# One copy of each pixel instead of two: VectorE takes the odd columns of every patch, and the edge columns move into the rows of the other offsets

## The reference, cut to what matters

```
xs = jnp.concatenate([x] + [_shift(x, s) for s in shifts], axis=1)     # five copies, 15 channels
t = xs ... reshape(B, h * w, PATCH * PATCH * C5)
tn = (t - mu) * jax.lax.rsqrt(var + EPS) * ln_gamma + ln_beta
h = jnp.einsum('bnp,pd->bnd', tn, W) + b
h = jnp.concatenate([h, text], axis=1)                                 # 228 tokens
h = h + attention(layernorm(h)); h = h + ffn(layernorm(h))
```

## Time and profile before

| | |
|---|---|
| median of 3 runs | 1894.72 us (1888.71 to 1895.52) |
| the profiled execution | 1889.4 us, span 1887.7 us |
| mean granted TensorE clock | 0.88 |
| PE busy | 1579.8 us (84%) |
| PEld busy | 1297.6 us (69%) |
| DVE busy | 1364.8 us (72%) |
| ACT busy | 1283.7 us (68%) |
| POOL busy | 1089.7 us (58%) |
| patch matmuls that read `pix` (L1092) | 2048 instructions, 408.4 us |
| DMA | 132.96 MB, of which 118.32 MB read from HBM |

### The profile page before, as it was taken

How to read it: one execution, slowest core, us unless ns; L and a number is a source line. 1 busy time by engine, 2 the same in 40 slices (tenths; PEclk the granted TensorE clock), 3 DMA queues, 4 the chain that set the end, 5 groups by cost and what they waited for, 6 DMA issues and landing times.

```text
span 1887.7 us, 50796 instructions
## 1 busy us (share of the span) xinstructions
PE 1579.8 (84%) x16574; PEld 1297.6 (69%) x16574; DVE 1364.8 (72%) x3151; ACT 1283.7 (68%) x1958; POOL 1089.7 (58%) x1503
## 2 busy tenths in 40 slices
PE   0539999999999999999999999999466666666666
PEld 0427788888888888888888888887345555555555
DVE  3636676767767676767676767676389999999996
ACT  1226666766767676767676666665288888888887
POOL 5035555555555555555555555554177777777775
PEclk9869999999999999999999999999666666666665
DMA  8674666665657565756565666660000000000000
GB/s 102 141 127 59 95 87 96 86 99 83 103 79 104 83 99 83 99 88 94 89 94 91 91 93 88 94 87 25 17 16 21 21 21 22 22 22 22 22 22 26
DMA packets 159967, 132.96 MB, mean 70 GB/s; under 512 B 32558, under 2 KB 151040, under 8 KB 159808
## 3 DMA queue, kind: packets, MB, share of 16 engines
q1 hardware_dynamic: 159168, 131.00, 44.4%
q0 software_dynamic: 768, 1.57, 0.5%
HBM read 118.32 MB, written 11.91 MB: 69 GB/s over the span
## 4 chain that ended last, share of the span: by engine, by line
PE 66%; DVE 15%; issue 7%; SPq 3%; ACT 3%; DMA 3%; POOL 1%; DVEq 1%; ACTq 0%; POOLq 0%
PE ps L1092 20%; PE ps L1176 8%; PE ps L1259 7%; PE ps L1250 7%; PE ps L1206 4%; DVE ff_st L860 4%; PE ps L1238 3%; PE ps L1232 3%; PE ps L1211 3%; PE ps L1336 2%; PE ps L1355 2%; DVE xpix L841 2%; PE ps L1167 2%; DVE xpix L853 1%; PE ps L1157 1%
## 5 line engine op out<-in xcount | busy, mean ns | idle before, releaser
L1092 PE MATMUL ps<-w_eff,pix 118*112 118x193 f32 (+1 forms) x2048 | 408.4, 337 | 25.0 <-ACT pix L909 24.3
L927 ACT ACTIVATE probs<-ps,isw 116x688 f32<-116x688 f32 x384 | 299.2, 831 | 171.6 <-PE ps L1238 171.6
L527 POOL TENSOR_TENSOR xpix<-probs,g_b 112x192 f32<-112x192 f32 (+1 forms) x512 | 296.5, 609 | 109.1 <-ACT probs L1044 99.7
L741 DVE TENSOR_REDUCE nmax<-ps 116x12 bf16<-116x1344 f32 (+2 forms) x192 | 299.6, 1560 | 80.2 <-PE ps L1211 77.7
L452 POOL TENSOR_TENSOR xsq<-xsq 118x784 f32<-118x784 f32 (+2 forms) x192 | 221.8, 1155 | 218.5 <-ACT xsq L920 208.4
L1092 PEld LDWEIGHTS ps<-w_eff,pix 118*112 118x112 f32 (+1 forms) x2048 | 309.8, 167 | 52.4 <-issue 18.9
L472 POOL TENSOR_SCALAR_AFFINE_SELECT probs<-probs 116x464 f32<-116x464 f32 x384 | 268.2, 717 | 46.5 <-ACT probs L927 31.0
L909 ACT ACTIVATE pix<-xpix 118x896 f32<-118x896 f32 (+1 forms) x128 | 198.4, 1552 | 104.9 <-DMA xpix<-in_x 56.0
L457 POOL TENSOR_TENSOR front_st<-front_st,expo 128x2 f32<-128x2 f32 x64 | 45.0, 703 | 235.2 <-DVE front_st L693 221.2
L1336 PE MATMUL ps<-w1t,xpix 96*112 96x384 f16 (+1 forms) x512 | 160.7, 488 | 14.6 <-ACT xpix L1035 13.3
L685 DVE TENSOR_SCALAR front_st<-ps 112x1 f32<-112x1 f32 (+1 forms) x128 | 18.3, 151 | 213.8 <-PE ps L1157 202.4
(11 more groups left out here) (161 smaller groups left out, 3363.3 us busy)
## 6 DMA issues: line engine op xcount, KB each, us to landing
xpix<-in_x SPq DMA_DIRECT2D x192, 196.0 KB
xpix<-in_x SPq DMA_DIRECT2D x192, 195.1 KB
rden<-den_rows SPq DMA_DIRECT2D x256, 85.5 KB, 2.1
out<-xpix SPq DMA_DIRECT2D x64, 87.0 KB
out<-xpix SPq DMA_DIRECT2D x64, 84.0 KB
xpix<-in_x SPq DMA_DIRECT2D x128, 34.1 KB
xpix<-in_x SPq DMA_DIRECT2D x128, 34.0 KB
den<-o_sb SPq DMA_DIRECT2D x256, 2.7 KB
```

What stands on the lines that cost most here:

```text
L527: last = nc.gpsimd.tensor_tensor(v2[0:P, b, tile, cols], gel[0:P, b, tile, cols], g2_b[0:P, cols], ALU.mult)
L741: V.tensor_reduce(dst, src, AX_X, ALU.max, negate=True).then_inc(s_mx, 1)
L927: A(probs[0:TB, g, 2 * e:2 * e + 2, :], ps[0:TB, 4 + 2 * e:6 + 2 * e, 0:SK], ACT.Exp, scale=isw[0:TB, 7:8]).then_inc(s_p, 1)
L1092: last = MM(ps_tok[tile][0:P, :], src, w_eff[0:HI, o, :], start=(o == 0), stop=(o == OFFS - 1))
```

## The change

- **Loads.** Each pixel is loaded once: `load_pixels` issues five DMAs instead of ten. Both images' pixels share one tensor `xpix`, the even image in partitions 0 to 53 and the odd one in 64 to 117 (`UP` = 64).
- **Regrouping.** `pix` is two buffers in turn. ACT copies the even columns to rows 0 to 53 (`regroup_even`, the same two shapes of 8 x 112 and 8 x 84 elements in each partition), and DVE the odd columns to rows 64 to 117 (new `regroup_odd`, one copy of 8 x 196 = 1568 elements in each partition, behind maxima round 2). Both are for image n+4 in step n; ACT's copy of tile 1 moves from the start of the next step to behind copy_maxima.
- **Edges.** The 2 x 48 edge pixels of a patch no longer have an offset of their own. POOL gathers them in one copy (`sides`, 48 partitions x 2 x 182), now at the end of its step for image n+4, and two SP DMAs (`place_sides`) put them into six further rows of each half of `pix` (`EDGE` = 6, 6 rows x 8 offsets = 48). A matmul has 124 rows, and an image has 8 offsets x 2 tiles, 32 instructions; P4 goes from 14 to 13 (of 16). ACT has one square less (L917), POOL one add less (`ADDS` = 3).
- **Broadcast.** The inverse denominators go to 17 rows of each head's 32 instead of 32; `rden` is filled with ones once.
- **Start-up.** The scratch of the setup moves out of `xpix`, so image 1 is loaded right behind image 0; DVE's setup gets the odd copy of image 0 (behind the patch weights, before READY1) and, behind the text rows, that of image 1. The edge weights are moved by two DMAs.

```diff
-OFFS = PATCH // 2 + 1
-LO, HI = CH * (PATCH + 2), 64 + CH * (PATCH + 2)
+OFFS = PATCH // 2
+LO, UP = CH * (PATCH + 2), 64
+EDGE = CH * PATCH // OFFS
+HI = UP + LO + EDGE
...
-        xpix = [sb(f"xpix{i}", [128, GRID * SIDE]) for i in range(2)]
-        side = [sb(f"side{i}", [128, IMG_TOK]) for i in range(2)]
+        xpix = sb("xpix", [128, GRID * SIDE])
+        side = sb("side", [128, 2, IMG_TOK])
...
-        pix = sb("pix", [128, 8, IMG_TOK])
+        pix = sb("pix", [128, 2, OFFS, IMG_TOK])
...
-                for first, col in ((0, 0), (64, 1)):
-                    for c in range(CH):
-                        sp.dma_start(buf[first + PATCH * c:first + PATCH * (c + 1), :, 0:SIDE - col],
-                                     rows[c][:, :, col:]).then_inc(s_x[par], 16)
...
+                for c in range(CH):
+                    sp.dma_start(buf[base + PATCH * c:base + PATCH * (c + 1), :, :], rows[c]).then_inc(s_x[par], 16)
...
+            def place_sides(m, par):
+
+                sp.wait_ge(s_side, m + 1)
+                for half, shift in ((0, 1), (1, 0)):
+                    row = UP * half + LO
+                    sp.dma_start(pix[row:row + EDGE, par, :, shift:IMG_TOK],
+                                 side[UP * par:UP * par + CH * PATCH, half, 0:IMG_TOK - shift]).then_inc(s_place, 16)
...
             sp.wait_ge(s_pad, 3)
             load_pixels(0, 0)
+            load_pixels(1, 1)
...
-                    sp.dma_start(rden[32 * j:32 * j + 32, :, :].rearrange("p g k -> p (g k)"),
-                                 src.partition_broadcast(32)).then_inc(s_sh, 16)
+                    sp.dma_start(rden[32 * j:32 * j + HD + 1, :, :].rearrange("p g k -> p (g k)"),
+                                 src.partition_broadcast(HD + 1)).then_inc(s_sh, 16)
...
+            def step_images(n, par, place=True, load=True):
+                turn_denominators(n)
+                if place:
+                    place_sides(n + 4, par)
                 if load:
-                    next_pixels(n + 3, par)
+                    next_pixels(n + 3, 1 - par)
...
-                after(pool, s_lrstd, m - 1)
+                after(pool, s_place, 32 * m)
+                rows = slice(UP * par, UP * par + CH * PATCH)
+                pixels = xpix[rows, :].rearrange("p (h w) -> p h w", h=GRID)[:, :, PATCH - 1:SIDE - 1]
                 apart(pool)
-                nc.gpsimd.tensor_copy(edge[0][0:LO, :, 1:GRID], src[0:LO]).then_inc(s_side, 1)
...
+                nc.gpsimd.tensor_copy(side[rows, :, :].rearrange("p s (h w) -> p s h w", h=GRID)[:, :, :, 0:GRID - 1],
+                                      pixels.rearrange("p h (w e) -> p e h w", e=PATCH)[:, 0:2]).then_inc(s_side, 1)
...
-                                                  (xsq[0:HI, 0, :], xsq[0:HI, 0, :], xsq[0:HI, 1, :]),
-                                                  (ssq_sb[0:HI, :], xsq[0:HI, 0, :], xsq[0:HI, 8, :]))):
+                                                  (ssq_sb[0:HI, :], xsq[0:HI, 0, :], xsq[0:HI, 1, :]))):
...
-                if newest:
-                    sides(n + 3, par, count)
...
                 if newest:
                     add_squares(n + 3)
+                if coming is not None:
+                    sides(n + 4, par, coming)
...
+            def regroup_odd(m, par, count):
+
+                dve.wait_ge(s_x[par], 16 * XDMA * count)
+                dve.wait_ge(s_sq, m - 1)
+                rows = slice(UP * par, UP * par + LO)
+                apart(dve)
+                V.tensor_copy(pix[UP:UP + LO, par, :, :],
+                              xpix[rows, :].rearrange("p (t m e) -> p e m t", m=8, e=2)[:, 1]).then_inc(s_odd, 2)
...
                 if new:
                     maxima(n + 1, 2)
+                if coming is not None:
+                    regroup_odd(n + 4, 1 - b, coming)
...
-            def regroup(m, par, count, tile):
+            def regroup_even(m, par, count, tile):
...
-                after(act, (s_half, s_front)[tile], m)
                 if tile == 0:
-                    after(act, s_sq, m)
-                pixels = xpix[par][0:HI, :].rearrange("p (t m e) -> p e m t", m=8, e=2)[:, 0]
-                A(pix[0:HI, :, lo:lo + P], pixels[:, :, lo:lo + P], ACT.Copy).then_inc(s_pix, 1)
+                    after(act, s_front, m - 1)
+                    after(act, s_sq, m - 1)
+                pixels = xpix[UP * par:UP * par + LO, :].rearrange("p (t m e) -> p e m t", m=8, e=2)[:, 0]
+                A(pix[0:LO, par, :, lo:lo + P], pixels[:, :, lo:lo + P], ACT.Copy).then_inc(s_pix, 1)
...
-                if newest:
-                    regroup(n + 3, par, count, 1)
...
                 if coming is not None:
-                    regroup(n + 4, 1 - par, coming, 0)
+                    regroup_even(n + 4, 1 - par, coming, 0)
                 if new:
                     copy_maxima(n + 1)
+                if coming is not None:
+                    regroup_even(n + 4, 1 - par, coming, 1)
...
-                    if o < 8:
-                        src = pix[0:HI, o, lo:lo + P]
-                    else:
-                        src = side[par][0:HI, lo:lo + P]
...
-            P1, P2, P3, P4 = 2, 4, 9, 14
+            P1, P2, P3, P4 = 2, 4, 9, 13
```

More of the change, by code:

```diff
@@ L39 @@
 EPS_LN, EPS_RMS = 1e-5, 1e-6
-READY1, READY2 = 36, 52
+READY1, READY2 = 35, 51
 N_W = HIDDEN * DIM
@@ L344, in load_pixels @@
             def load_pixels(n, par):
-                buf = xpix[par][:, :].rearrange("p (h w) -> p h w", h=GRID)
+                base = UP * par
+                buf = xpix[:, :].rearrange("p (h w) -> p h w", h=GRID)
                 rows = x[bass.ds(n, 1)].rearrange("a c (h i) w -> (a c) i h w", i=PATCH)
-                for first, col in ((0, 0), (64, 1)):
-                    for c in range(CH):
-                        sp.dma_start(buf[first + PATCH * c:first + PATCH * (c + 1), :, 0:SIDE - col],
-                                     rows[c][:, :, col:]).then_inc(s_x[par], 16)
[L353 to L356, removed]
+                for c in range(CH):
+                    sp.dma_start(buf[base + PATCH * c:base + PATCH * (c + 1), :, :], rows[c]).then_inc(s_x[par], 16)
+                sp.dma_start(buf[base + 48:base + 51, 1:GRID, :],
+                             rows[:, PATCH - 1, 0:GRID - 1, :]).then_inc(s_x[par], 16)
+                sp.dma_start(buf[base + 51:base + 54, 0:GRID - 1, :],
+                             rows[:, 0, 1:GRID, :]).then_inc(s_x[par], 16)
+            def place_sides(m, par):
[4 more added lines that the diff above has]
+                                 side[UP * par:UP * par + CH * PATCH, half, 0:IMG_TOK - shift]).then_inc(s_place, 16)
             sp.wait_ge(s_pad, 3)
             load_pixels(0, 0)
+            load_pixels(1, 1)
+            sp.wait_ge(s_weff, 1)
+            for half, col in ((0, 0), (1, PATCH + 1)):
+                row = UP * half + LO
+                sp.dma_start(w_eff[row:row + EDGE, :, 0:DIM], wacc[0:CH * PATCH, col, :]).then_inc(s_wmove, 16)
+            place_sides(0, 0)
+            place_sides(1, 1)
             sp.wait_ge(s_vset, V_SETUP)
@@ L423, in _ @@
                 nc.gpsimd.memset(clear, 0.0).then_inc(s_zero, 1)
-            for clear in (xpix[0][:, :], side[0][:, :], side[1][:, :]):
+            for clear in (xpix[:, :], side[:, :, :], pix[:, :, :, :]):
                 nc.gpsimd.memset(clear, 0.0).then_inc(s_pad, 1)
@@ L477, in _, with step_images @@
             sides(0, 0, 1)
[L478 to L480 removed]
+            sides(1, 1, 1)
             add_squares(0)
[L483 removed]
+            def step_images(n, par, coming, old=True, newer=True, newest=True):
                 if newer:
@@ L591, in _ @@
             inner = wacc[0:LO, 1:17, :].rearrange("p (m e) d -> p m e d", e=2)
-            step(V.tensor_copy(w_eff[0:LO, 0:8, 0:DIM], inner[:, :, 0, :]))
-            step(V.tensor_copy(w_eff[64:HI, 0:8, 0:DIM], inner[:, :, 1, :]))
-            step(V.tensor_copy(w_eff[0:LO, 8, 0:DIM], wacc[0:LO, 0, :]))
-            step(V.tensor_copy(w_eff[64:HI, 8, 0:DIM], wacc[0:LO, 17, :]))
             dve.sem_inc(s_weff, 1)
+            for e in range(2):
+                step(V.tensor_copy(w_eff[UP * e:UP * e + LO, :, 0:DIM], inner[:, :, e, :]))
+            dve.sem_inc(s_weff, 1)
+            dve.wait_ge(s_x[0], 16 * XDMA)
+            step(V.tensor_copy(pix[UP:UP + LO, 0, :, :],
+                               xpix[0:LO, :].rearrange("p (t m e) -> p e m t", m=8, e=2)[:, 1]))
+            dve.sem_inc(s_odd, 2)
             dve.wait_ge(s_zero, 5)
@@ L1401, in shape_constants @@
     mult = np.zeros((128, OFFS), np.float32)
-    mult[0:LO, 0:8] = count[:, 1:17:2]
-    mult[64:HI, 0:8] = count[:, 2:17:2]
-    mult[0:LO, 8], mult[64:HI, 8] = count[:, 0], count[:, 17]
-    assert (mult[:, 1:7] == mult[:, 1:2]).all()
+    for half, col in ((0, 0), (1, PATCH + 1)):
+        row = UP * half + LO
+        mult[UP * half:row] = count[:, 1 + half:17 + half:2]
```

(2 more changed lines are left out.)

161 lines of the change are left out of this document (79 added, 82 removed).

## The result

The changed kernel takes 2487.52 us (median of 4 runs, 2485.03 to 2491.31) against 1893.51 us before: the ratio is 1.314, with a 95% interval of 1.311 to 1.318. I had forecast 1846 us, so the prediction missed by 642 us and in sign.

The account below looks back on a forecast made before the run. PE was taken as full, with DVE's chain equally long up to maxima round 2. From the profiled 1889.4 us, 35 (PE) and 9 (start-up) were subtracted: 1845, stated as 1846 us; range 1832 to 1880.

Parts of the forecast that it names:

- the part on DMAs: DMAs and SP's queue: five loads for ten, two edge DMAs and the narrower broadcast, all put at nothing.
- DVE's copy: Odd-column copy behind maxima round 2: 1.9 us, bounds 0.97 and 3.5, hidden in DVE's idle time.
- PE, four instructions fewer: PE's patch matmuls, 32 an image instead of 36: 0.70 us removed, net 0.57 us a step, 35 us in all.
- The 0.13 us of new wait: At turn_maxima, PE starting earlier would wait for maxima round 2: 0.13 us a step, between nothing and 0.34.
- the cover: DVE's idle time before the next front that hides its copy: 3.26 us less PE's 0.57, so 2.69 us.
- The rival of the slow copy: DVE's copy takes 3.5 us, exceeds its idle time and lengthens the step by 0.24 us: 1900 us; chance 0.12.
- The port: Rival: POOL's `sides` wins the shared port, DVE's copy starts 1.0 us late, 0.35 us a step net: 1859 us; chance 0.15.
- POOL and ACT: POOL's side copy at most 0.99 us, cost nothing; ACT's exps 0.2 us late, hidden by 1.2 us.
- Start-up: Early loading of both images brings square_turn of image 1 from 134.36 to about 125 us: 9 us gained, bounds 4 and 13.

Follow-up runs that it names:

- runs 3 and 4: The changed kernel with the broadcast to 18 and to 31 rows a head instead of 17: 1839.15 us and 2850.72 us (one run).
- run 7: The changed kernel with 32 broadcast rows and DVE's copy of the odd columns done a second time into an unread buffer: 1895.49 us, ratio 0.9985.
- run 1: The changed kernel with the broadcast back to 32 rows a head instead of 17: 1837.85 us, ratio 0.971 to the kernel before.
- run 9: The changed kernel with 32 broadcast rows and image 1 loaded only behind the text rows, as in the kernel before: 1843.19 us, ratio 0.970.
- run 8: The changed kernel with 32 broadcast rows and two patch instructions moved ahead of score round 2 (P3, P4 = 10, 14): 1839.34 us, ratio 0.968.
- run 10: The changed kernel with 32 broadcast rows and DVE's odd copy reading a dense stretch (wrong pixels): 1841.93 us, one run, ratio 0.969.

## Why the prediction was wrong

**The step that failed** is in the part on DMAs: "The narrower broadcast ends a transfer for which DVE does not wait. All nothing." The trace of before told that the transfer was hidden; I took this as proof that changing it costs nothing, since fewer bytes can only be quicker. The cover was small. In the step shown before, the four transfers are issued from 676.59 to about 678.3 us, a transfer lands 2.2 us behind its issue, so the last one at about 680.5, and DVE starts the multiplication at 680.96: from first issue to use there are 4.4 us. From first issue to landing the broadcast took some 3.9 us, and in the changed kernel it takes 13.2. That leaves a wait of 13.2 - 4.4 = 8.8 us, close to the mean that the waits of the changed kernel show (185.8 / 21 = 8.8); the step shown there has 9.48. So the term put at nothing was 28.46 - 17.98 = 10.5 us a step, this wait and PE's slower clock behind it. I had bounds for DVE's copy and none for this edit, which changed the shape of a transfer for which no row of before existed; by the same standard it needed one. Had the whole gone to one engine, an estimate from the widths alone (2.2 us times up to 16) would have shown the danger. The rule cited with runs 3 and 4 speaks against 17 rows, and the prediction made no use of it.

**PE, four instructions fewer: right, undersized.** Forecast 0.57 us a step, measured with 32 rows:

```profile
L1188 PE MATMUL ps<-ones,ssq_sb x244: 213/226/259, 165.9 to 1244.8; 124*112 124x1 f32 x61, 124*84 124x1 f32 x61
```

(1244.8 - 165.9) / 60 = 17.98, so 18.73 - 17.98 = 0.75 us. The 0.13 us of new wait did not come:

```profile
702.64 1.54 PE L1123 MATMUL ps<-w_eff,pix 124*84 124x193 f32 x8
704.02 0.32 PE L1251 MATMUL ps<-ident_b,nmax 116*128 116x116 bf16 x3
704.18 1.17 PE L1123 MATMUL ps<-w_eff,pix 124*84 124x193 f32 x6
705.28 0.36 PE L1263 MATMUL ps<-aux,maskc 32*116 32x344 bf16 x4
```

```profile
702.88 1.05 DVE L761 TENSOR_REDUCE nmax<-ps 116x4 bf16<-116x912 f32 x1
703.96 1.50 DVE L779 COPY pix<-xpix 54x1568 f32<-54x1568 f32 x1
706.49 0.16 DVE L705 TENSOR_SCALAR front_st<-ps 112x1 f32<-112x1 f32 x1 [1.03 <-PE ps L1188]
```

turn_maxima starts at 704.02, 1.38 us after its eight matmuls began and 0.09 behind the end of the maxima (703.93): DVE and PE meet there to within a tenth. From the scores at 665.75 to those at 678.26 PE took 12.51 us in the step of the earlier trace rows; in the step from 711.45 to 723.26 it takes 11.81. That is 0.70 us, all that the prediction had as removed. Over 60 periods the gain is 45 us. (One count in this part of the prediction is wrong: ahead of score_round 2 stand 18 instructions, nine offsets, and not 20. No sum uses it.)

**DVE's copy: hidden, as forecast,** at 1.49 us and not 1.9. The factor that ACT pays for the stride (1.96) was too much for DVE (1.54, over the whole instruction). The dense row of ACT in it reads PSUM; its squares, which read SBUF densely, give nearly the same (1262 ns for 1176 elements, 464 for 196: 0.81 ns for each further one, a factor of 2.0). The rest of the cover is 1.03 us, and run 7 shows the price of more. The rival of the slow copy (3.5 us) was far from true, but its price was about right: run 7, with 3.6 us for both copies, came to 1895 us where the rival said 1900, and its step is 0.18 us longer than the one before where the rival said 0.24. In part that is luck: the cover was 0.16 us smaller than forecast and PE's gain 0.18 us larger.

**The port.** DVE wins in the changed kernel (705.66 against 705.92 for POOL), and POOL, which nobody waits for, pays.

**POOL and ACT:** nothing is late on either with 32 rows; the side copy takes 1.88 us with its wait, where I had 0.99.

**Start-up: smaller, and not by the mechanism forecast.** square_turn of image 1 moved from 134.36 us to 130.27 in run 1, so 4.1 us where I said 9 (125). The first steady one moved from 172.54 to 165.95, 6.6 us; some 1.5 of these are the two steps in between at 0.75 each. The setup did not end 1.5 us earlier but 4 us later in run 1, at 115.45 - 11.01 = 104.4: image 0's pixels were not there at 72.4 but at 74.7, and DVE's setup stood behind them.

```profile
74.67 1.47 DVE L612 COPY pix<-xpix 54x1568 f32<-54x1568 f32 x1 [6.37 <-DMA xpix<-in_x]
```

```profile
115.45 1.48 DVE L822 COPY pix<-xpix 54x1568 f32<-54x1568 f32 x1 [11.01 <-DMA h_all<-probs]
```

The prediction left out what the loads of image 1 take from those of image 0. By run 9 the early load gains nothing on balance. What made the 4.1 us (fewer bytes in the queue, fewer patch matmuls) was not taken apart.

**The sum** with 32 rows: 45 + 6.6 = 51.6 us; the profiled executions are 1889.4 and 1838.31 us, 51.1 apart. So the forecast for all edits but one was 1845 and came to 1838; PE's part was 10 us too small, start-up's some 2 us too large. That one edit, put at nothing, cost 650 us.

## What to carry to other kernels

- A transfer that is hidden is not one that may be changed freely. For each transfer whose shape changes, ask over how many engines it is spread, in both patterns, and how long it may take until somebody waits: here 17 rows in place of 32 saved 47% of the bytes, their packets took 11.2 us in place of 2.1, and 18 rows cost nothing.
- When every engine is less busy than before and one wait fills the difference, undo the edit that touches the awaited tile before anything else: one run settled 650 us.
- The DMA share of a stretch in which one transfer runs tells over how many engines it is spread: 0.06 to 0.07 is one of sixteen.
- Loads issued early can stand in the way of what was issued just before them (run 9): ask what they delay as well as what they hasten.
- A step that is closed by three engines to within a tenth of a microsecond gives what is taken out of its gap, and gives nothing when work is only moved inside it (run 8).

## What the runs showed of the hardware

- Broadcasts from DRAM to 17 and to 31 rows of 2736 bytes, four at a time: 2.4 us and 0.41 us a row, 26.6 GB/s together, one packet at a time at a DMA share of 0.06; to 18 rows up to nine packets at a time, to 32 rows sixteen, 2.1 us from issue to landing, and the same time of the kernel for both.
- Two loads of 3 partitions at the end of an image's loads: 2.0 to 3.3 packets at a time in the mean.
- A DVE copy in f32 with a step of 64 bytes: 1496 ns for 1568 elements, dense 972. ACT's factor for the same step, by further elements, was 1.96.
- A DVE copy of this kind and a POOL copy do not run side by side: 0.6 us of waiting on DVE in one order (run 7), 0.5 us less on POOL when DVE's copy ahead of it is 0.5 us shorter (run 10).
- After some 9 us without work PE's granted clock was 0.50 (1.2 GHz), and its twelve f32 projection matmuls took 4.18 us in place of 2.21.
